# Four graph layers on one core: pass 2 and 3 write their messages in source order and sum them with matmuls, where they were added into DRAM tables

## The reference, cut to what matters

```python
# layer 0: an MLP per edge, summed by dst
h = relu(concat([x[dst], x[src], edge_attr_32]) @ W1 + b1);  out = segment_sum(h @ W2 + b2, dst)
# layer 1: features scaled by out-degree, summed by dst; a node without edges keeps its own features
agg = segment_sum(x[src] * ci[src], dst) * cj;  h = where(in_deg > 0, agg, x);  out = relu(h @ W.T + b)
# layer 2: summed by src (row = src, col = dst)
agg = segment_sum(dis[row] * dis[col] * x[col], row);  out = relu(agg @ W.T + b)
# layer 3: a gate per edge, summed by src
gate = silu(edge_attr_40 @ W1.T + b1) @ W2.T + b2 + sum(emb[type[src]] * (emb[type[dst]] @ adaptW.T))
msg = gate * x[dst] * (cw(edge_weight) * node_vec[dst])
x + segment_sum(msg, src) / clip(segment_sum(node_vec[dst], src)), then a layernorm with gamma and beta
```

## Time and profile before

| | |
|---|---|
| time, median of 3 runs | 21880.12 us (21870.0 to 21891.17) |
| span of the profiled execution | 21878.8 us, 1.3 us under that median; no other time of that execution is given |
| granted TensorE clock | 1.00 in every stretch (2.4 GHz, the upper of the two levels) |
| busy share of the span | POOL 77%, PE 46%, DVE 37%, ACT 10% |
| first to last indirect DMA, pass 0, 1, 2, 3 | 4819, 3975, 5848, 6017 us |

### The profile page before, as it was taken

How to read it: one execution, slowest core, us unless ns; L and a number is a source line. 1 busy time by engine, 2 the same in 40 slices (tenths; PEclk the granted TensorE clock), 3 DMA queues, 4 the chain that set the end, 5 groups by cost and what they waited for, 6 DMA issues and landing times. The chain is left out here.

```text
span 21878.8 us, 262731 instructions
## 1 busy us (share of the span) xinstructions
PE 10000.2 (46%) x60516; PEld 8854.9 (40%) x60517; DVE 8115.0 (37%) x22720; ACT 2278.4 (10%) x4904; POOL 16830.2 (77%) x12521
## 2 busy tenths in 40 slices
PE   5666666665111111144444444444344444444442
PEld 4666666665111111144444444444333333333332
DVE  2555555553333333321111111111344444444444
ACT  1000000000000000000000000000122222222221
POOL 3888888884777777748888888888488888888886
DMA  3333333332222222223333333333344444444443
GB/s 95 83 82 82 83 82 83 82 82 85 50 46 47 46 46 46 47 32 34 36 36 36 35 36 36 34 36 36 60 55 56 58 55 59 55 55 59 55 55 60
DMA packets 2063013, 1225.51 MB, mean 56 GB/s; under 512 B 1752244, under 2 KB 1901172, under 8 KB 2059927
## 3 DMA queue, kind: packets, MB, share of 16 engines
q0 software_dynamic: 1150320, 489.05, 22.0%
q1 hardware_dynamic: 432932, 593.16, 9.4%
q10 hardware_dynamic: 479744, 143.12, 2.9%
HBM read 965.61 MB, written 258.57 MB: 56 GB/s over the span
## 5 line engine op out<-in xcount | busy, mean ns | idle before, releaser
L1114 POOL DMA_INDIRECT sum<-l_msg,l_uring x6250 | 9913.1, 1586 | 2012.5 <-issue 1798.0
L457 POOL DMA_INDIRECT l_rows<-btab,l_sd x3125 | 3867.3, 1238 | 1266.3 <-issue 1266.0
L817 POOL DMA_INDIRECT l_rows<-y,l_sd x3125 | 3012.0, 964 | 1017.1 <-issue 951.5
L1271 PE MATMUL ps<-l_rows,l_same 128*128 128x48 f32 x6250 | 1439.6, 414 | 3011.9 <-ACT l_msg L1337 3008.8
L1271 PEld LDWEIGHTS ps<-l_rows,l_same 128*128 128x128 f32 x6250 | 1370.6, 330 | 3080.9 <-issue 2395.4
L889 PE MATMUL ps<-l_ohe,l_rows 128*48 128x32 f32 x6250 | 604.2, 269 | 3427.2 <-DVE l_ohe L846 1843.9
L1155 DVE TENSOR_SCALAR l_oht<-l_dstb,l_nid 32x640 f32 (+1 forms) x1250 | 588.7, 500 | 3896.0 <-ACT l_rows L1324 3781.8
L889 PEld LDWEIGHTS ps<-l_ohe,l_rows 128*48 128x48 f32 x6250 | 537.6, 192 | 3493.8 <-issue 1859.9
L587 PE MATMUL ps<-l_rhs,l_lhs 64*128 x6250 | 1468.5, 427 | 970.3 <-DVE l_rows L530 731.1
L587 PEld LDWEIGHTS ps<-l_rhs,l_lhs 64*128 64x128 f32 x6250 | 1360.1, 328 | 1068.9 <-issue 1068.9
L1246 PE MATMUL ps<-l_eat,l_w 80*96 x1250 | 949.2, 884 | 1435.8 <-ACT l_sil L1330 1211.9
(11 more groups left out here) (204 smaller groups left out, 12655.6 us busy)
## 6 DMA issues: line engine op xcount, KB each, us to landing
l_srcb<-ids SPq DMA_DIRECT2D x375, 800.0 KB, 4.7
sum<-l_msg,l_uring POOLq DMA_INDIRECT x6250
l_dstb<-ids SPq DMA_DIRECT2D x376, 200.0 KB
l_eat<-in_ea40P SPq DMA_DIRECT2D x125, 600.0 KB
l_lhs<-in_ea32T ACTq DMA_DIRECT2D x625, 80.0 KB, 2.1
l_rows<-btab,l_sd POOLq DMA_INDIRECT x3125, 2.5
esrc<-l_rows ACTq DMA_DIRECT2D x625, 80.0 KB, 2.0
l_rows<-y,l_sd POOLq DMA_INDIRECT x3125, 2.4
```

Source lines behind the costliest of these rows:

```text
L457: pool.indirect_dma_start(rows[:, t, :], None, d["btab"], bass.IndirectOffsetOnAxis(ap=sd[:, t, 0:1], axis=0)).then_inc(gat[c], 16)
L817: pool.indirect_dma_start(rows[:, t, :], None, d["y1"], bass.IndirectOffsetOnAxis(ap=sd[:, t, 0:1], axis=0)).then_inc(gat[c], 16)
L1114: pool.indirect_dma_start(sums[k], bass.IndirectOffsetOnAxis(ap=uring[:, t:t + 1], axis=0), msg[:, t, :], None, compute_op=ALU.add).then_i ...
L1271: done = t.matmul(comb[c % 2][:, j, :], equal, rows[:, c * CT + j, :], start=True, stop=True)
```

## The change

Most of the kernel is rewritten. By what the prediction speaks of:

1. **Pass 0, operands.** The row of counts 0 to 127 that every one-hot is compared with (`iota_row`, `iota_row_bf` in SBUF) is copied once to PSUM (`count_row`), and so are the node ids `nid` of a window. `one_hot` is a two-source comparison now (`tensor_tensor` with `nid` broadcast from PSUM) instead of a `tensor_scalar`. The edge features of a group come in one DMA instead of five. Degrees are counted per position in the chunk and per part of the run (`hist`, 6 parts).
2. **Pass 1** makes three more things for each group. `uidx` is now a unique place for every edge: its rank among the edges of the same block of 128 src nodes, from two cumulative-count matmuls a chunk (`count_on`) and a product and a sum on DVE. The gates of layer 3 are made here (hidden and gate matmuls, silu on ACT) and stored in DRAM (`gates`). And a share of the table `order` is filled with zeros by a DMA. The comparison of all sources (L862) is gone.
3. **Passes 2 and 3.** `same` and the sum within a tile are gone. POOL's indirect DMA writes `msg` rows (49 values and the low digit of src) without adding into `order`, each to its own place. The groups are cut into parts of 40, 28, 20, 15, 12 and 10. From group 40 on, each "reading" group also reads back a step of 40 tiles of the parts already written, four blocks of 10 (`ordb`); DVE makes 4 one-hots of 1280 columns (`block_digits`), PE does 40 fp32 matmuls (`block_reduce`), DVE adds 40 results of 49 columns to `agg` in SBUF (`block_sums`), at places it loads into registers, 10 at a time, each ten in a line of 64 bytes. 94 steps are needed and 85 groups read, so 9 steps are left for a tail after the last scatter; there the values are split into three bf16 parts, with work on ACT and POOL.
4. **Prologue and epilogues.** The node tables are made within the prologue. The epilogues work in runs of 10 blocks, with steps of one run beside those of another, and take sums straight from SBUF; the 5 DRAM tables are gone. `epilogue0` does one matmul a block instead of three.

The diff, cut to its core:

```diff
@@ pass0, vector @@
             def one_hot(g, c):
-                v.tensor_scalar(lhs[0:WN, chunk_edges(c)], dstb[:, ds((g % 2) * GE + c * CE, CE)], nid[:, c:c + 1], None, ALU.is_equal).then_inc(oht_ready, 1)
+                v.tensor_tensor(lhs[0:WN, chunk_edges(c)], bc(nid[:, c:c + 1], [WN, CE]), dstb[:, ds((g % 2) * GE + c * CE, CE)], ALU.is_equal).then_inc(oht_ready, 1)
...
-                    v.tensor_tensor(hlo[:, c, :, :], bc(r["iota_row_bf"][:, None, :], [P, CT, P]),
+                    v.tensor_tensor(hlo[:, c, :, :], bc(count_row[:, None, :], [P, CT, P]),
...
@@ pass0, scalar @@
-                for c in range(NCH):
-                    act.wait_ge(hid_ready, g * NCH + c + 1)
-                    act.nop(nofuse=True)
-                    act.dma_start(lhs[WN:KW, chunk_edges(c)], a["ea32T"][:, ds((g * GT + c * CT) * P, CE)]).then_inc(eat_in[c], 16)
+                act.wait_ge(hid_ready, g * NCH + NCH)
+                act.nop(nofuse=True)
+                act.dma_start(lhs[WN:KW, :], a["ea32T"][:, ds(g * GE, GE)]).then_inc(eat_in, 16)
@@ pass1, tensor @@
+                hidden(0)
+                hidden(1)
+                for c in range(NCH):
+                    pe.wait_ge(hot_ready, g * NCH + c + 1)
+                    count_on(c, earlier).then_inc(cum_ready, 1)
+                    gates(c)
...
+                    pe.wait_ge(cum_read, g * NCH + c + 2)
+                    count_on(c, notearlier).then_inc(rank_done, 1)
+                    if c + 2 < NCH:
+                        hidden(c + 2)
@@ scatter_pass, gpsimd @@
-                        pool.indirect_dma_start(sums[k], bass.IndirectOffsetOnAxis(ap=uring[:, t:t + 1], axis=0),
-                                                msg[:, t, :], None, compute_op=ALU.add).then_inc(sc[k], 16)
+                        pool.indirect_dma_start(d["order"], bass.IndirectOffsetOnAxis(ap=uring[:, t:t + 1], axis=0),
+                                                msg[:, t, :], None).then_inc(sc[c], 16)
@@ scatter_pass, vector @@
+            def block_digits(n, b):
+                lo = ordb[b][:, :, MW:OW]
+                dve.wait_ge(ord_in[b], (n + 1) * 16)
+                v.tensor_tensor(ohs[b][:, :, :], bc(count_row[:, None, :], [P, RB[b], P]), bc(lo, [P, RB[b], P]), ALU.is_equal).then_inc(ohs_ready, 1)
+            def block_sums(n, b):
...
+                places = load_places(dve, "place", pl, r, blk, n, first[b], RB[b])
+                dve.wait_ge(red_ready, n * len(RB) + b + 1 + len(RB))
+                for k in range(RB[b]):
+                    nth = first[b] + k
+                    dve.wait_ge(agg_added, n * RT + nth + (RT + 1 if nth else RT + 2))
+                    cols = agg[:, ds(places[k] + (nth % 2) * WIDE, MW)]
+                    v.tensor_tensor(cols, cols, red[b % 2][:, k * MW:(k + 1) * MW], ALU.add).then_inc(agg_added, 1)
@@ scatter_pass, tensor @@
+            def block_reduce(n, b):
...
+                for k in range(RB[b]):
+                    done = t.matmul(red[b % 2][:, k * MW:(k + 1) * MW], ohs[b][:, k, :],
+                                    ordb[b][:, k, 0:MW], start=True, stop=True)
```

More of the change, by code:

```diff
@@ L485, in _ @@
                 one_hot(0, c)
-            with dve.Fori(0, NG) as g:
+            for part in range(PARTS):
+              with dve.Fori(pl.begin[part], pl.begin[part] + GROUPS[part]) as g:
                 starts, rounds, before, last = load_group(dve, "dve", pl, r, g)
@@ L878, in _ @@
             pe.sem_inc(row_free, 5)
-            with pe.Fori(0, NG) as g:
-                _starts, rounds, before, _last = load_group(pe, "pe", pl, r, g)
+            pe.sem_inc(rank_done, 5)
+            pe.sem_inc(z_ready, 2 * NCH)
+            pe.sem_inc(lone_turned, 1)
+            pe.wait_ge(ones_set, 2)
+            pe.wait_ge(hist_in, 16)
+            for q in range(PARTS):
+                for j in range(CT):
+                    done = t.matmul(totals[q], ones[:, :], hist[:, q, j * NB:(j + 1) * NB], start=(j == 0), stop=(j == CT - 1))
@@ L893, in _ @@
                     pe.sem_inc(acc_ready, 1)
+            for lo, hi, part in segments:
+                if lo == pl.begin[part]:
+                    pe.wait_ge(first_set, 1)
+                    pe.wait_ge(cum_read, pl.begin[part] * NCH + 1)
+                    t.matmul(cum, ones[0:1, :], bc(last_tile[0:1, part:part + 1, :], [1, CT, NB]), start=True, stop=False, skip_group_check=True)
+                    for j in range(1, CT):
+                        t.matmul(cumf[:, j * NB:CT * NB], ones[:, :], hist[:, part, 0:(CT - j) * NB], start=False, stop=False, skip_group_check=True)
+                with pe.Fori(lo, hi) as g:
+                    group(g, hi <= NB)
@@ L1144, in _, with group @@
+            def group(g, reading, late, head):
+                n = g - READ0
                 _starts, rounds, before, last = load_group(dve, "dve", pl, r, g)
@@ new lines, in group @@
+                if not gated:
+                    dve.wait_ge(edge_in, (g + 1) * 16)
+                    dve.wait_ge(logit_made, g + 1)
+                if late:
+                    block_sums(n - 1, LAST)
+                for c in range(NCH):
+                    take(c)
+                    if reading and not head and c <= LAST:
+                        block_digits(n, c)
+                dve.wait_ge(look_taken, (g + 1) * NCH)
+                dve.sem_inc(group_done, 1)
+                if not gated:
+                    v.tensor_reduce(r["adapt"][:, ds(g * GT, GT)], prod[:, :, :], AX, ALU.add).then_inc(logit_made, 1)
@@ new lines, in group @@
+                if reading and head:
+                    block_digits(n, 0)
+                    for b in range(LAST):
+                        block_digits(n, b + 1)
+                        block_sums(n, b)
+                elif reading:
+                    for b in range(LAST):
+                        block_sums(n, b)
+            with dve.Fori(0, READ0) as g:
+                group(g, False, False, False)
+            for part in range(1, PARTS):
+                begin = pl.begin[part]
+                with dve.Fori(begin, begin + 1) as g:
+                    group(g, True, part > 1, True)
+                with dve.Fori(begin + 1, begin + GROUPS[part]) as g:
+                    group(g, True, True, False)
@@ new lines, in last_reduce @@
+            def last_reduce(n, b):
+                pe.wait_ge(ohs_ready, n * len(RB) + b + 1)
+                pe.wait_ge(lo_made, (n - TAIL0) * len(RB) + b + 1)
+                pe.wait_ge(agg_added, n * RT + RT + 2 + (first[b - 1] if b >= 2 else first[b + 2] - RT if b == 0 else 0))
+                for k in range(RB[b]):
+                    for i in range(3):
+                        done = t.matmul(red[b % 2][:, k * MW:(k + 1) * MW], ohsb[b][:, k, :],
+                                        parts[b][:, i, k, :], start=(i == 0), stop=(i == 2))
+                done.then_inc(red_ready, 1)
@@ new lines, in _ @@
+        @block.gpsimd
+        def _(pool):
+            g = nc.gpsimd
+            for c, (b, k) in enumerate(runs):
+                g.tensor_tensor(both[:, b:b + k, :], sums[0][:, b:b + k, 0:F], sums[1][:, b:b + k, 0:F], ALU.add).then_inc(both_ready, 1)
+            pool.wait_ge(mult_set, 1)
+            for c, (b, k) in enumerate(runs):
+                pool.wait_ge(normed, c + 1)
+                g.tensor_tensor(ht[:, b:b + k, 0:F], x[:, b:b + k, :], per_block(r["mult"][:, b:b + k], k), ALU.mult).then_inc(y_ready, 1)
@@ L1413, in _ @@
[L1413 to L1428 removed]
+            act.wait_ge(eps_set, 1)
@@ new lines, in _, with join, shape @@
+            sp.wait_ge(o_out, stores * 16)
+        @block.gpsimd
+        def _(pool):
+            g = nc.gpsimd
+            def join(c):
+                b, k = runs[c]
+                g.tensor_tensor(both[:, b:b + k, :], sums[0][:, b:b + k, :], sums[1][:, b:b + k, :], ALU.add).then_inc(both_ready, 1)
+            def shape(c):
+                b, k = runs[c]
+                hs = h[:, b:b + k, :]
+                pool.wait_ge(normed, c + 1)
+                g.tensor_tensor(hs, hs, bc(gam[:, None, :], [P, k, F]), ALU.mult).then_inc(self_g, 1)
+                pool.wait_ge(self_g, c + 1)
+                g.tensor_tensor(hs, hs, bc(bet[:, None, :], [P, k, F]), ALU.add).then_inc(affine, 1)
+            pool.wait_ge(w_in, 32)
+            for c in range(n):
+                join(c)
+            for c in range(n):
+                shape(c)
```

1765 lines of the change are left out of this document (1084 added, 681 removed).

## The result

| | before | changed |
|---|---|---|
| time, median of 3 runs | 21880.12 us | 16730.78 us (16729.72 to 16737.95) |
| ratio | 1 | 0.7647, 95% interval 0.7634 to 0.7661 |
| span of the profiled execution | 21878.8 us | 16728.8 us |

The forecast was 16,790 us with a range of 16,400 to 17,850. Four, marked "first chip", ran where the kernel before took 21,894 us.

The account below looks back on a forecast made before the run. POOL's list of indirect DMAs was taken to bound all four passes. Passes 3940 + 3955 + 3975 + 4018, tails 356 and intervals 540 sum to 16,784 us, stated as 16,790 us, range 16,400 to 17,850.

Parts of the forecast that it names:

- What bounds the kernel: All four passes: POOL's own list is the path, 3125 x (duration of one DMA + 0.30 us) a pass.
- Term 1: Passes 2 and 3: 6250 scatters without the addition fall from 1.586 us to the gather's 0.944, 4025 us less.
- Term 2: Pass 0: with one input in PSUM the long gathers go; 3940 us instead of 4819, 879 us less.
- Rival C: Pass 0: the long gather stays, its cause not being the SBUF input; 911 us stay, 17,700 us; chance 0.09.
- Pass 1: Pass 1: PE's added work, 21 us a group, stays hidden by POOL; 3955 us instead of 3975.
- Reading groups: Passes 2 and 3: a loop of 30 to 31 us, 0.7 us charged to each of 85 groups; 3975 and 4018 us.
- Tails: After the last scatter of passes 2 and 3: nine steps of 17.5 us, DVE the chain; 356 us in all.
- Intervals: Prologue with tables and four epilogues: 200, 90, 75, 70 and 105 us, 540 in sum instead of 1218.
- Rival A: Passes 2 and 3: DVE or PE becomes the bound of the reading groups; 17,300 to 17,850 us; chance 0.17.
- Rival B: Passes 2 and 3: a plain scatter costs what the adding one did, 1.54 us; 20,370 us; chance 0.07, in-between prices included.
- D: Reading groups: the 40 dependent additions crawl, about 1.1 us each, making the kernel slower, above 21,900 us; chance 0.02.

Follow-up runs that it names:

- Experiment 1: Changed kernel with the addition put back into its 6250 indirect DMAs (first chip): 20,340.7 us, ratio to the kernel before 0.9291.
- experiment 2: Kernel before with the addition taken out of its 6250 indirect DMAs and nothing else (first chip): 18,529.5 us, ratio 0.8464.
- experiment 3: Changed kernel with the count row of pass 0's ten out-degree digit one-hots read from SBUF again (first chip): 17,544.9 us, ratio to the kernel before 0.8014.
- experiment 5: Changed kernel with the count row of the ten out-degree digits read from the fp32 row in SBUF: 23,733 us, ratio 0.9841, on a slower chip.

## Why the prediction was right

**What bounds the kernel: right.** POOL's list did in all passes, before and after: each pass is 3125 x (mean duration + 0.30) within 25 us, but for pass 3 of the kernel before, which lies 62 us above.

**Term 1, the scatter without the addition: mechanism right, size 4% off.** I took the gather's 0.944 us; it is 0.969, so 6250 x 0.025 = 156 us were lacking. (6250 x 0.642 is 4012 us, not the 4025 I wrote. Neither stands in the sum, which goes by 1.252 us a DMA with its interval, 0.008 above 0.944 + 0.30; there 106 us were lacking.) Experiment 1 prices the addition by itself at 3610 us in the changed kernel, experiment 2 at 3364 in the one before. The rest of what passes 2 and 3 gave (3902 us from 11,867 to 7965) are the long scatters and the waits that went with the five tables and with `same`.

**Term 2, pass 0: right, and for the reason given.** 856 us came off where 879 were forecast, and experiment 3 brings back 814 by one operand alone. Rival C has fallen. So has the remark, marked as inferred, that `tensor_tensor` doesn't hold up descriptor generation (the Trainium skill, "SBUF — State Buffer", section "Who interferes with whom"): the 7.13 us row contradicts it with a bf16 count row, the 7.2 us of experiment 5 with an fp32 one. The rule of the same section on two inputs in SBUF agrees with both, and with the 1.4 us that is the longest gather of pass 0 now.

**Pass 1: right.** 3940 us where 3955 were forecast, PE busy 21.5 us a group (forecast 21), though much of it at the lower clock level.

**Reading groups: the step that failed, to the good.** I put passes 2 and 3 at 62 and 106 us above 3125 x 1.252, for the reading groups' loop, the heads and contention; they lie 13 and 20 us above 3125 x 1.269. The terms themselves were right: PE 28.5 us (forecast 28 to 29.5), an addition 0.21 us (0.17 to 0.32), a digit one-hot 1.48 (1.47). What I took for a loop of 30 to 31 us that adds to POOL's stayed beneath it. This error of 135 us and the 106 that the dearer scatter cost in the same two forecasts (6250 x 0.017) nearly cancel. That the passes came out right to 28 us is luck, and not because every term was.

**Tails: 307 instead of 356.** A step is 16.1 us, not 17.5, since the loads mostly run beside the one-hots; DVE is the chain, as said.

**Intervals: 554 instead of 540**, each within 20 us of its estimate.

**Rival A (DVE or PE binds the reading groups)** did not happen in the measured result. Nor do the rows bear out 2 us for a load: ten registers take 1.07 us (L1355). My own bound was too high as well, since of the 1.47 us at a group's start the load is only 0.60. But PE has only 3.4 us of 31.9 free, and on the two other chips something of this kind did happen, see below. **Rival B** is excluded by the row of L1507, **D** by 0.21 us an addition.

**Not foreseen:** the granted clock, which the forecast of PE's work took to stay at 1.00 without a word; and that the gain depends on the chip.

## What to carry to other kernels

When POOL issues a long list of indirect DMAs, count them and read the duration of one: adding into DRAM costs 1.55 us against 0.97 here, and half the rows save only 0.07, so fewer and plain DMAs are worth much work on engines that have time. Read the maximum beside the median: single long ones point at a burst of another engine. Moving one operand to PSUM removed them here, and the ten comparisons took the same 0.80 and 0.65 us as before. And measure on more than one chip: here the whole gain is there on one and gone on another, for a reason that the runs don't show.

## What the runs showed of the hardware that I had not expected

**On two other chips the gain is gone.** There the kernel before took 24,093 to 24,121 us, 10% more, and the changed kernel, on one of them, 24,284, 45% more than its 16,731 and 0.7% more than the kernel before. All passes grew: pass 0 from 3963 to 6114 us, pass 1 from 3940 to 5490, passes 2 and 3 with what lies between them from 8208 to 12,037. So it is not that the added work took PE's slack: in pass 0 PE is busy 3143 us, less than the 3305 of the kernel before. The durations of POOL's DMAs and of PE's matmuls are what they were. The timeline of PE in pass 0 (changed kernel, slower chip) shows where the time is:

```profile
2977.80 7.25 PE L645 MATMUL ps<-l_ohe,l_hid 128*128 128x32 f32 x33
2985.80 0.21 PE L645 MATMUL ps<-l_ohe,l_hid 128*128 128x32 f32 x1 [0.75 <-issue]
2988.59 0.21 PE L645 MATMUL ps<-l_ohe,l_hid 128*128 128x32 f32 x1 [2.58 <-issue]
2991.39 0.21 PE L645 MATMUL ps<-l_ohe,l_hid 128*128 128x32 f32 x1 [2.59 <-issue]
...
3026.99 7.68 PE L645 MATMUL ps<-l_ohe,l_hid 128*128 128x32 f32 x35
3035.03 0.21 PE L645 MATMUL ps<-l_ohe,l_hid 128*128 128x32 f32 x1 [0.36 <-issue]
3037.81 0.21 PE L645 MATMUL ps<-l_ohe,l_hid 128*128 128x32 f32 x1 [2.57 <-issue]
```

At nearly the same place in each turn of the loop, 49.2 us apart, PE gets nine or ten matmuls singly, 2.1 to 2.8 us from one to the next, and waits for nothing; some 22 us pass, then it runs on at full pace. POOL meanwhile issues its gathers, then waits 18 us for the ids (`l_sd`), because all that follows on PE is late. Experiment 5 ran beside it, with a gather of 7.2 us in each group; there the same 50 records are one piece, but PE waits later:

```profile
3008.72 10.88 PE L645 MATMUL ps<-l_ohe,l_hid 128*128 128x32 f32 x50
...
3046.12 6.76 PE L630 MATMUL ps<-l_rhs,l_lhs 64*128 x30 [18.32 <-DVE l_rows L566]
```

```profile
3010.78 7.19 POOL L489 DMA_INDIRECT l_rows<-btab,l_sd  x1 [0.30 <-issue]
...
3032.91 0.18 DVE L528 CAST l_dcolf<-l_sd 128x25 f32<-128x25 int32 x1 [9.18 <-issue]
```

So the slow stretch of PE goes where POOL is held up beside it, and another takes part of its place: DVE stands 9.2 us at "issue" where it stood 2.0 on the first chip, while POOL issues gathers again. A turn takes 45.7 us instead of 49.2 (31.7 on the first chip), and pass 0 took 5572 us instead of 6114 although its gathers took 867 us more. In the stretches read, the lateness falls mostly where POOL issues one indirect DMA after another.

One guess is that the instructions themselves arrive late. The Trainium skill ("Runtime: NRT & Kernel Launch", section "Instruction fetch mechanics") says that each sequencer fetches its instructions by its own DMA queue, that this is mostly hidden, and that a taken branch to a page that is not held stalls. The same place in each turn would agree with such a stall. But the trace shows no fetch: its queues of kind "instruction" have 93 packets in the whole run on either chip, and none from 2250 to 3550 us of the slower one, 26 turns of this loop. The cause stays open. So does why these chips do it and the first did not, and why the kernel before lost only 10% there, for no trace of it was taken on them; no version with shorter loops was tried.

**Rows are nearly free, the addition is not.** A scatter of 64 rows took 0.895 us of POOL, one of 128 rows 0.969, one of 128 adding rows 1.546, with 144 packets instead of 32.

**The granted clock fell and came back only for moments.** It was 1.00 through pass 0 (PE busy 79%) and the interval behind it. Then PE stood 17.8 us, ran 60 fp32 records without a stop (8.67 us from 4241) and stood 5.3 us again, and from 4252 on the clock was at 0.50. It was 1.00 once more from 4262 to 4275, and for 4 to 14 us each at 5515, 6395, 7027 and 7877, every time right after the long records of a new part (L1218 and L1220, 5.6 us without a stop). After 7890 it stayed at 0.50, even in the first 40 groups of pass 2 where PE is busy a third of the time. In the kernel before it stayed at 1.00 throughout. What decides between the two, these rows don't show. The same instructions on either side, PE in pass 1 of the changed kernel:

```profile
4264.47 0.37 PE L1183 MATMUL ps<-l_hot,l_earlier 128*128 128x490 bf16 x1
4271.46 1.98 PE L1208 MATMUL ps<-l_ohe,l_rows 128*48 128x32 f32 x40
...
4299.50 0.61 PE L1183 MATMUL ps<-l_hot,l_earlier 128*128 128x490 bf16 x1
4301.60 3.41 PE L1208 MATMUL ps<-l_ohe,l_rows 128*48 128x32 f32 x40
```

The matmul with 490 columns and the short sums take 1.6 to 1.7 times as long at the 1.2 GHz level. But 50 records of the look-up L1683 take 10.95 us at it, where 10.90 stood at the 2.4 GHz level. The block matmuls L1659 (49 columns) take 414 ns each in the mean at the lower level, and the nearest of the kernel before, L1271 (48 columns), 414 at the upper. So the two kinds that fill PE in the reading groups don't feel the clock. In pass 1, where others do, POOL waited only 44 us in all for other engines, so the fall can't have cost that pass much; what it cost the intervals, no run tells.
